# Float32r stacks written by the transfers themselves instead of staged and copied by ScalarE, in a six-attention kernel

## Chip, cores and metric

One NeuronCore of a Trainium2 chip runs the whole kernel. The metric is device time in microseconds (us), the median of several executions. 16 sequences (`B`) of 256 tokens with 256 features go through six attention blocks, 0 to 5, one after the other.

## What is computed

Each block has 16 heads of width 16. In block 0 the scores of queries and keys get two masks; blocks 1, 4 and 5 are plain; block 2 is causal; blocks 2 and 3 count, per head, the non-zero scores of query 0 and mask all keys from that count on (the penalty). The core of blocks 2 and 3 in the reference:

```python
energy = jnp.einsum('bhsk,bhtk->bhst', Q, K)
lengths = jnp.sum(energy[:, :, 0, :] != 0, axis=-1)
energy = jnp.where(cols[None, None, None, :] >= lengths[:, :, None, None], -jnp.inf, energy)
if causal:
    energy = jnp.where(cols[None, :] > cols[:, None], -jnp.inf, energy)
score = jax.nn.softmax(energy / jnp.sqrt(jnp.asarray(dk, energy.dtype)), axis=-1)
out = jnp.einsum('bhst,bhtk->bhsk', score, V) * m
```

Around each attention stand projections of queries, keys and values, a residual sum and a layer norm; blocks 1 and 5 have a feed-forward part of width 1024, block 3 one of width 256.

## The kernel before

**Units and steps.** A unit `n` (0 to 95) is one sequence in one block: block `n // 16`, sequence `n % 16`. One global order of steps, made by `plan()` from the tables `PRE` and `POST` (lines 69 to 110) and sorted by time, is followed by all engines: each walks through `win.order` and does its own part of every entry. Time in the tables is counted in steps, eight to a unit, relative to the unit's start `8 * n`; a negative entry is done while earlier units attend. In step `p` of unit `n` stand `nat` of head pair `p` (scores with queries on the partitions, from which VectorE takes the row maximum, L1018) and `st` of the pair seven steps earlier (transposed scores, of which ScalarE takes the exponential into `pt`, L854). `pvg` (L690) multiplies four pairs by the values. The score banks `ps_nat` and `ps_st` exist once each, so a `nat` waits for the last maximum, an `st` for the last exponential. All else shares the three banks of `ps_misc`; `Order` gives each entry a bank, and a bank is taken again only when its reader has emptied it.

**Queries and keys of blocks 1 to 5.** The scores use float32r operands in stacks `q_st` and `k_st`, double-buffered by unit parity, of 64 rows for each head of a pair: every fourth row (`STEP`) a high part, the next ones high and low parts, so that one product gives near float32 precision; of the rows left over, one holds the penalty (`PEN_R`), two the negated row maximum as high and low part (`HI_R`, `LO_R`), which ScalarE's input then has subtracted already. They are made so:

- `pq` and `pk` (L619): projection into a `ps_misc` bank, held until the low part is out.
- ScalarE rounds the bank into `upper` (L801, L804), VectorE writes the remainder into `lower` (`pql`, `pkl`; L955, L958).
- `qin` and `kin`: SyncE issues three transfers of 256 KB each (L439), which place the parts into the staging areas `raw_q`, `raw_k`, float32. There is one staging area each, so `qin` of a unit waits for the copy of the unit before (L435, L437).
- `pen` (L452): the penalty rows, computed by VectorE in `len` from the small product `e0` (L629), go to `raw_k` by two transfers.
- `qcp` and `kcp` (L814, L826): ScalarE copies each staging area into the stack, in two halves of four pairs, and so rounds to float32r. `nat` waits for them (L492, L493).
- `nmt`: the transposed maxima; GpSimd issues two small transfers into rows `HI_R` and `LO_R` of `q_st` (L1130, L1132).

`upper` and `lower` exist once; the `upper` of a unit waits until the transfers of the unit before have read it (L796). The staging areas lie in slots 1 and 2 of `qk0`, which block 0 uses for its own queries and keys, so that the first `row`, `qin` and `kin` of block 1 wait for unit 14 (L422).

## Time and profile before

| | us |
|---|---|
| median of 3 runs | 2823.91 (2817.97 to 2825.75) |
| the profiled execution, own time | 2822.13 |
| its span, first to last instruction | 2820.3 |
| PE busy in the span | 2653.0 |
| VectorE (DVE) busy | 1816.7 |
| ScalarE (ACT) busy | 1554.2 |

PE is TensorE's matmul side and PEld its weight loads; a busy share counts instructions in flight. SPq is SyncE's queue, which only issues transfers. "PEclk" is the granted share of TensorE's full clock. In a listing, "[x <-y]" is idle time x of the engine before the row and what ended it. Between its own time and its span the profiled execution has 1.8 us.

### The profile page before, as it was taken

The numbers are of one execution on the slowest core, as the hardware profiler recorded it, in microseconds if no ns is written. First come the engines' busy times: TensorE is split into PE (matmuls) and PEld (weight loads), VectorE is DVE, ScalarE is ACT, GpSimd is POOL, SyncE is SP. The second block draws the span as 40 slices with busy tenths as digits, with TensorE's granted clock in tenths as the row PEclk, the third lists the DMA queues.
The fourth block names the chain that finished last, engine by engine and source line by source line (L and its number), as shares of the span: only waits on it lengthen the run. The fifth ranks groups of instructions, "written<-read, shape, count | busy, mean of one in ns | idle before, by whom it ended". The sixth has DMA issues, their size and how long they took to land.

```text
span 2820.3 us, 57005 instructions
## 1 busy us (share of the span) xinstructions
PE 2653.0 (94%) x22720; PEld 1958.1 (69%) x22720; DVE 1816.7 (64%) x3629; ACT 1554.2 (55%) x2129; POOL 749.8 (27%) x838
## 2 busy tenths in 40 slices
PE   7999999899999999999998889889999989999999
PEld 5777777567777777766666666666666667777777
DVE  5566666465555565666668888888677775555552
ACT  1333333365555554566656666666676676666653
POOL 0011111133333332332323444554222221111111
PEclk9999999899999999999999999999999999999999
DMA  2210000121111111122222222122322221111210
GB/s 92 81 45 29 25 25 21 57 81 65 54 54 54 54 47 47 55 93 71 79 77 89 85 70 69 64 70 77 107 70 80 71 81 58 62 62 62 73 47 16
DMA packets 138362, 177.67 MB, mean 63 GB/s; under 512 B 51747, under 2 KB 58547, under 8 KB 138036
## 3 DMA queue, kind: packets, MB, share of 16 engines
q1 hardware_dynamic: 92022, 171.25, 16.9%
q0 software_dynamic: 46080, 2.79, 1.2%
q8 instruction: 184, 3.01, 0.4%
q14 instruction: 76, 0.62, 0.1%
HBM read 40.13 MB, written 4.19 MB: 16 GB/s over the span
## 4 chain that ended last, share of the span: by engine, by line
PE 82%; DVE 9%; ACT 5%; issue 3%; DMA 1%; SPq 0%; POOL 0%; ACTq 0%; DVEq 0%
PE ps_pv L690 10%; PE ps_nat L517 10%; PE ps_misc L749 9%; PE ps_misc L619 9%; PE ps_st L538 8%; PE ps_misc L771 7%; PE ps_misc L645 6%; PE ps_misc L722 4%; DVE mx L1018 4%; ACT pt L854 3%; PE ps_nat L521 2%; PE ps_misc L701 2%; PE ps_st L542 2%; PE ps_misc L614 2%; PE ps_misc L739 2%
## 5 line engine op out<-in xcount | busy, mean ns | idle before, releaser
L854 ACT ACTIVATE pt<-ps_st 128x1024 f32<-128x1024 f32 (+1 forms) x768 | 758.5, 988 | 616.3 <-PE ps_st L542 288.9
L1018 DVE TENSOR_REDUCE mx<-ps_nat 128x4 f32<-128x1024 f32 x640 | 781.0, 1220 | 413.4 <-PE ps_nat L517 267.5
L538 PE MATMUL ps_st<-q_st,k_st 64*128 64x256 f32 (+1 forms) x2560 | 326.1, 333 | 69.9 <-ACT pt L854 66.6
L538 PEld LDWEIGHTS ps_st<-q_st,k_st 64*128 64x128 f32 x2560 | 194.8, 188 | 249.7 <-issue 184.9
L690 PE MATMUL ps_pv<-pt,vaug 128*32 128x256 f32 (+1 forms) x6144 | 361.0, 376 | 0.0
L517 PE MATMUL ps_nat<-k_st,q_st 64*128 64x256 f32 (+1 forms) x2560 | 273.8, 290 | 40.9 <-DVE mx L1018 34.6
L1156 POOL TENSOR_TENSOR rstd<-var,half_pow 128x2 f32<-128x2 f32 x144 | 103.1, 716 | 726.3 <-DVE var L905 724.6
L749 PE MATMUL ps_misc<-xF,weights 128*128 128x256 f32 x1152 | 281.3, 387 | 1.8 <-ACT xF L868 1.5
L1130 POOL DMA_DIRECT2D q_st<-negm_hi x160 | 97.7, 611 | 690.3 <-DVE negm_hi L1028 690.3
L1164 POOL TENSOR_TENSOR xn<-xn,tiles 128x512 f32<-128x512 f32 x128 | 163.8, 1280 | 412.7 <-DVE xn L909 412.4
L690 PEld LDWEIGHTS ps_pv<-pt,vaug 128*32 128x32 f32 x6144 | 179.6, 110 | 123.1 <-issue 10.6
L517 PEld LDWEIGHTS ps_nat<-k_st,q_st 64*128 64x128 f32 x2560 | 202.2, 190 | 60.3 <-DVE mx L1018 23.9
L749 PEld LDWEIGHTS ps_misc<-xF,weights 128*128 128x128 f32 x1152 | 209.8, 190 | 47.2 <-issue 12.3
L771 PE MATMUL ps_misc<-weights,hT 128*128 128x256 f32 x1024 | 240.9, 382 | 0.0
L619 PE MATMUL ps_misc<-xT,weights 128*128 128x256 f32 x896 | 229.2, 400 | 1.8 <-ACT xT L871 0.9
L876 ACT ACTIVATE hT<-ps_misc,cols 128x256 f32<-128x256 f32 x288 | 121.0, 471 | 166.7 <-PE ps_misc L749 166.6
L771 PEld LDWEIGHTS ps_misc<-weights,hT 128*128 128x128 f32 x1024 | 188.5, 190 | 27.8
L619 PEld LDWEIGHTS ps_misc<-xT,weights 128*128 128x128 f32 x896 | 169.6, 198 | 31.2 <-ACT xT L871 4.8
L860 ACT ACTIVATE ote<-ps_pv 128x512 f32<-128x512 f32 x192 | 114.7, 598 | 123.8 <-PE ps_pv L690 123.7
L814 ACT ACTIVATE q_st<-qk 128x1024 fp32r<-128x1024 f32 x160 | 168.6, 1054 | 23.7 <-PE ps_st L538 12.8
L826 ACT ACTIVATE k_st<-qk 128x1024 fp32r<-128x1024 f32 x160 | 169.1, 1057 | 8.5 <-issue 8.5
L1165 POOL TENSOR_TENSOR xn<-xn,tiles 128x512 f32<-128x512 f32 x128 | 163.8, 1280 | 10.0
(117 smaller groups left out, 4082.3 us busy)
## 6 DMA issues: line engine op xcount, KB each, us to landing
qk<-upper SPq DMA_DIRECT2D x320, 256.0 KB, 2.5
qk<-lower SPq DMA_DIRECT2D x160, 256.0 KB, 2.6
weights<-in_weights SPq DMA_DIRECT2D x19, 512.0 KB, 4.7
cT<-in_ctx_t SPq DMA_DIRECT2D x32, 256.0 KB, 2.8
cn<-in_ctx SPq DMA_DIRECT2D x32, 256.0 KB, 2.7
xT<-in_x_t SPq DMA_DIRECT2D x16, 256.0 KB, 2.9
xn<-in_x SPq DMA_DIRECT2D x16, 256.0 KB, 2.7
out<-xn SPq DMA_DIRECT2D x16, 256.0 KB, 3.1
```

The costliest lines, as they stand in the source:

```text
L517: return nc.tensor.matmul(ps_nat[:, j, hf, 0:keys], lhs, rhs, start=hf == 0, stop=last)
L538: return nc.tensor.matmul(ps_st[:, j, kh, 0:S - q0], lhs, rhs, start=kh == first, stop=last)
L619: last = nc.tensor.matmul(bank[:, j * S:(j + 1) * S], wv[:, dk, j * P:(j + 1) * P], src[:, dk, :], start=dk == 0, stop=dk == 1)
L645: last = nc.tensor.matmul(bank[:, hf * D:(hf + 1) * D], src[:, dk, hf * P:(hf + 1) * P], wv[:, dk, :], start=dk == 0, stop=dk == 1)
L690: last = nc.tensor.matmul(ps_pv[32 * j:32 * j + 32, c, q0:S], vaug[:, rot, kh, s, :], pt[:, at_p, s % 2, kh * S:(kh + 1) * S - q0], start= ...
L749: last = nc.tensor.matmul(bank[:, c * S:(c + 1) * S], wu[:, dk, ch * P:(ch + 1) * P], xF[:, dk, :], start=dk == 0, stop=dk == 1)
L771: last = nc.tensor.matmul(bank[:, th * D:(th + 1) * D], hT[:, ch, th * P:(th + 1) * P], wd[:, ch, :], start=part == 0 and ch == 0, stop=pa ...
L814: nc.scalar.activation(q_st[:, rot, 4 * i:4 * i + 4, :], raw_q[:, 4 * i:4 * i + 4, :], ACT.Copy).then_inc(q_stacked, 1)
L826: nc.scalar.activation(k_st[:, rot, 4 * i:4 * i + 4, :], raw_k[:, 4 * i:4 * i + 4, :], ACT.Copy).then_inc(k_stacked, 1)
L854: nc.scalar.activation(pt[:, g % PT_SLOTS, :, 0:used], ps_st[:].rearrange("p j a b -> p j (a b)")[:, :, 0:used], ACT.Exp, scale=SCALE).the ...
L1018: last = nc.vector.reduce_max(out, ps_nat[:], AX)
L1164: link(nc.gpsimd.tensor_tensor(x, x, tile2("g" + name), ALU.mult))
```

## The change

The staging areas, the copies `qcp` and `kcp` and the entries `row` are gone. `qin` and `kin` write straight into the stacks, each as two entries `i = 0, 1` of four head pairs (half a unit). For this the weights' column order (`by_slot`) is changed so that the even partitions of the projections belong to one half and the odd ones to the other. A half of `qin` is four transfers: 4 rows of zeros into `HI_R` and `LO_R` (now 31 and 63) and three of 128 KB; a half of `kin` is three of 128 KB. VectorE's low part is written as float32r. The penalty is also placed per half, two transfers each. From unit 18 on each half waits for the last `st` of the same half two units earlier, whose stack it overwrites. `upper` and `lower` become double-buffered and move into the slots of `qk0`. The constant rows of ones are loaded at the start into `hT` (two transfers of 256 KB) and written once to both buffers of both stacks. The maxima, the exponentials, the products and their shapes stay as they are. The tables `PRE` and `POST` are new throughout; here `PRE` of blocks 1 to 5:

```diff
 PRE = {
-    1: [("ldt", 0, -17.8), ("xtr", 0, -16), ("qin", 0, -12.6), ("pq", 0, -9.5), ("pql", 0, -9.45),
-        ("kin", 0, -8.45), ("pk", 0, -6.5), ("pkl", 0, -5.25), ("qcp", 0, -1), ("pvv", 0, -0.9),
-        ("kcp", 0, -0.15), ("qcp", 1, 1.2), ("kcp", 1, 1.5)],
-    2: [("xtr", 0, -15), ("pq", 0, -14), ("pql", 0, -13.7), ("qin", 0, -9.6), ("pk", 0, -9.3),
-        ("kin", 0, -9.1), ("pkl", 0, -9), ("pen", 0, -8.6), ("q0b", 0, -6.8), ("e0", 0, -5.8),
-        ("qcp", 0, -5.75), ("len", 0, -5.5), ("kcp", 0, -2.5), ("qcp", 1, -2.1), ("kcp", 1, 0.45),
-        ("pvv", 0, 0.5)],
-    3: [("ldn", 0, -20.3), ("xtr", 0, -14.8), ("ctr", 0, -14.3), ("pq", 0, -10.5), ("qin", 0, -9.95),
-        ("pql", 0, -9.7), ("kin", 0, -9.4), ("pk", 0, -9.15), ("pkl", 0, -8.8), ("pen", 0, -7.2),
-        ("q0b", 0, -7), ("e0", 0, -6.3), ("len", 0, -5.75), ("qcp", 0, -4.1), ("kcp", 0, -3.3),
-        ("qcp", 1, -1.7), ("kcp", 1, 1.1), ("pvv", 0, 1.5)],
-    4: [("xtr", 0, -12.4), ("pq", 0, -11.2), ("pql", 0, -9.8), ("qin", 0, -9.6), ("pk", 0, -9.4),
-        ("pkl", 0, -9), ("kin", 0, -7.35), ("qcp", 0, -6.1), ("kcp", 0, -2.6), ("qcp", 1, -1.6),
-        ("kcp", 1, 0.75), ("pvv", 0, 2.5)],
-    5: [("ldn", 0, -22.7), ("clnA", 0, -17.8), ("clnB", 0, -16.9), ("ctr", 0, -14.3), ("xtr", 0, -10.5),
-        ("pq", 0, -9.8), ("pql", 0, -9.7), ("pk", 0, -9.2), ("pkl", 0, -8.6), ("kin", 0, -6.4),
-        ("kcp", 0, -2), ("qin", 0, -1.35), ("qcp", 0, -1.2), ("pvv", 0, 0), ("kcp", 1, 1.1), ("qcp", 1, 3)],
+    1: [("ldt", 0, -17.8), ("xtr", 0, -15.95), ("pq", 0, -10.2), ("pql", 0, -9.8), ("pk", 0, -9.6),
+        ("pkl", 0, -8.6), ("kin", 0, -7.9), ("qin", 0, -4.3), ("kin", 1, -1.5), ("qin", 1, -0.6),
+        ("pvv", 0, 0.1)],
+    2: [("xtr", 0, -15), ("pq", 0, -10.5), ("pql", 0, -9.8), ("pk", 0, -9.8), ("q0b", 0, -9.3),
+        ("pkl", 0, -8.9), ("e0", 0, -8), ("len", 0, -7.2), ("qin", 0, -6), ("kin", 0, -5.4),
+        ("pen", 0, -4.9), ("qin", 1, -1.55), ("kin", 1, -1.5), ("pen", 1, -1.4), ("pvv", 0, 0.8)],
+    3: [("ldn", 0, -17.8), ("xtr", 0, -14.8), ("ctr", 0, -14.3), ("pq", 0, -10.7), ("pql", 0, -9.8),
+        ("pk", 0, -9.6), ("pkl", 0, -9.55), ("q0b", 0, -8.1), ("e0", 0, -8), ("len", 0, -7.2),
+        ("qin", 0, -5.5), ("pen", 0, -5.1), ("kin", 0, -2.6), ("kin", 1, -2.5), ("pen", 1, -2.4),
+        ("qin", 1, -2.3), ("pvv", 0, 1.5)],
+    4: [("xtr", 0, -13.6), ("pq", 0, -10.6), ("pk", 0, -9.6), ("pql", 0, -9.5), ("pkl", 0, -8.85),
+        ("kin", 0, -8.4), ("qin", 0, -6), ("qin", 1, -1.6), ("kin", 1, -1.5), ("pvv", 0, 1.5)],
+    5: [("ldn", 0, -23.7), ("clnA", 0, -18.1), ("clnB", 0, -17.9), ("ctr", 0, -14.3), ("xtr", 0, -12),
+        ("pq", 0, -10.5), ("pql", 0, -9.8), ("pk", 0, -9.6), ("pkl", 0, -8.9), ("qin", 0, -6.2),
+        ("kin", 0, -3.1), ("kin", 1, -1.5), ("qin", 1, 0.1), ("pvv", 0, 0.4)],
 }
...
+        if a == 4 and n % B < 2:
+            for i in range(2):
+                add(8 * n + 4 * i - 5, "pen", n, i)
```

`POST` has the same entries as before at times moved by at most 2.5 steps (block 2: `lnA` 19.2 to 21.7, `lnB` 22.55 to 23.1; block 3: `otr` 0 12.1 to 14.1, `lnB` 1 27.2 to 29.2, `ff1` 24 to 24.5; block 4: `opr` 21.2 to 20.3, `otr` 1 17.5 to 17.95). The buffers and SyncE's part:

```diff
-        raw_q, raw_k = qk0[:, 0, 1:3].rearrange("p r c s -> p (r c) s"), qk0[:, 1, 1:3].rearrange("p r c s -> p (r c) s")
-        lower = sb("lower", [P, 2, 2 * S])
-        bias_b = lower[:, 0].bitcast(BF16)
+        upper = qk0[:, 0, 1:3].rearrange("p r (k c) s -> p r k (c s)", k=2)
+        lower = qk0[:, 1, 1:3].rearrange("p r (k c) s -> p r k (c s)", k=2)
...
+                for c in range(2):
+                    sp.dma_start(hT[32 * c:32 * c + 32], t["rows"][c]).then_inc(rows_loaded, 16)
...
                     elif kind in ("qin", "kin"):
+                        if n >= B + 2:
+                            sp.wait_ge(st_done, nth(("st", n - 2, 4 * i + 3)))
+                        elif n == B and i == 0:
+                            sp.wait_ge(rows_in, 64)
+                        hi, lo = (part[i:P:2, rot, 0 if kind == "qin" else 1] for part in (upper, lower))
                         if kind == "qin":
                             wait_out(sp, ("pq", n, 0))
-                            dst, parts, done = raw_q, (upper[:, 0].bitcast(F32), upper[:, 0].bitcast(F32), lower[:, 0]), q_in[rot]
+                            dst, parts, done = q_st[:, rot, 4 * i:4 * i + 4].bitcast(F32), (hi, hi, lo), q_in[rot][i]
+                            if n == B and i == 0:
+                                sp.wait_ge(zeros_made, 1)
+                            sp.dma_start(dst[HI_R:P:LO_R - HI_R], zeros[:].unsqueeze(1).to_broadcast([4, 4, S])).then_inc(done, 16)
                         else:
                             wait_out(sp, ("pk", n, 0))
-                            dst, parts, done = raw_k, (upper[:, 1].bitcast(F32), lower[:, 1], upper[:, 1].bitcast(F32)), k_in[rot]
-                        if n == B:
-                            sp.wait_ge(st_done, nth(("st", B - 2, PAIRS - 1)))
-                        elif kind == "qin":
-                            sp.wait_ge(q_stacked, nth(("qcp", n - 1, 1)))
-                        else:
-                            sp.wait_ge(k_stacked, nth(("kcp", n - 1, 1)))
+                            dst, parts, done = k_st[:, rot, 4 * i:4 * i + 4].bitcast(F32), (hi, lo, hi), k_in[rot][i]
                         for part, src in enumerate(parts):
                             sp.dma_start(dst[part:P:STEP], src).then_inc(done, 16)
...
                     elif kind == "pen":
                         sp.wait_ge(pen_ready, nth(("len", n, 0)))
+                        if n >= B + 2:
+                            sp.wait_ge(st_done, nth(("st", n - 2, 4 * i + 3)))
                         for m in range(2):
-                            sp.dma_start(raw_k[PEN_R:P:GROUP, m:PAIRS:2], pens[SLOT * m:SLOT * m + 2 * QUADS]).then_inc(pen_in[rot], 16)
+                            sp.dma_start(k_st[PEN_R:P:GROUP, rot, 4 * i + m:4 * i + 4:2].bitcast(F32),
+                                         pens[SLOT * m + QUADS * i:SLOT * m + QUADS * i + QUADS]).then_inc(pen_in[rot][i], 16)
```

TensorE and ScalarE:

```diff
                     if attention(n) > 0 and p % 4 == 0:
-                        pe.wait_ge(q_stacked, nth(("qcp", n, p // 4)))
-                        pe.wait_ge(k_stacked, nth(("kcp", n, p // 4)))
+                        pe.wait_ge(q_in[n % 2][p // 4], placed("qin", n, p // 4))
+                        pe.wait_ge(k_in[n % 2][p // 4], placed("kin", n, p // 4))
+                        if ("pen", n, p // 4) in win.place:
+                            pe.wait_ge(pen_in[n % 2][p // 4], penned(n, p // 4))
...
-                        dst = upper[:, "pq pk".split().index(kind), :]
-
-                        if n > B and kind == "pq":
-                            act.wait_ge(q_in[(n - 1) % 2], placed("qin", n - 1))
-                            if count := nth(("q0b", n - 1, 0)):
+                        dst = upper[:, rot, "pq pk".split().index(kind)].bitcast(F32R)
+                        if n < B + 2:
+                            last_use = max(m for m in range(B) if m % ROT == 1 + rot)
+                            act.wait_ge(st_done, nth(("st", last_use, PAIRS - 1)))
+                        else:
+                            for h in range(2):
+                                if kind == "pq":
+                                    act.wait_ge(q_in[rot][h], placed("qin", n - 2, h))
+                                else:
+                                    act.wait_ge(k_in[rot][h], placed("kin", n - 2, h))
+                            if kind == "pq" and (count := nth(("q0b", n - 2, 0))):
                                 act.wait_ge(q0_ready, count)
-                        elif n > B:
-                            act.wait_ge(k_in[(n - 1) % 2], placed("kin", n - 1))
...
-                    elif kind == "qcp":
-
-                        if i == 0:
-                            act.wait_ge(q_in[rot], placed("qin", n))
-                            if n == B:
-                                act.wait_ge(rows_in, 32)
-                        if n >= B + 2:
-                            act.wait_ge(st_done, nth(("st", n - 2, 4 * i + 3)))
-                        nc.scalar.activation(q_st[:, rot, 4 * i:4 * i + 4, :], raw_q[:, 4 * i:4 * i + 4, :],
-                                             ACT.Copy).then_inc(q_stacked, 1)
-                    elif kind == "kcp":
-
-                        if i == 0:
-                            act.wait_ge(k_in[rot], placed("kin", n))
-                            if n == B:
-                                act.wait_ge(rows_in, 32)
-                            if ("pen", n, 0) in win.place:
-                                act.wait_ge(pen_in[rot], penned(n))
-                        if n >= B + 2:
-                            act.wait_ge(st_done, nth(("st", n - 2, 4 * i + 3)))
-                        nc.scalar.activation(k_st[:, rot, 4 * i:4 * i + 4, :], raw_k[:, 4 * i:4 * i + 4, :],
-                                             ACT.Copy).then_inc(k_stacked, 1)
```

## Rows read from the trace of the kernel before

**Rows 1.** Part 1 of the page, engine busy us (share) xinstructions:

```profile
PE 2653.0 (94%) x22720; PEld 1958.1 (69%) x22720; DVE 1816.7 (64%) x3629; ACT 1554.2 (55%) x2129; POOL 749.8 (27%) x838
```

**Rows 2.** Windows, one per block: stretch, us, busy by engine, PEclk, DMA share, GB/s:

```profile
48.20:557.30 509.10, 488.40 (x4843) 347.35 (x4843) 300.52 (x524) 174.75 (x207) 67.52 (x61) 0.98 0.13 41
557.30:1099.00 541.70, 521.57 (x3848) 393.89 (x3850) 324.78 (x616) 301.32 (x446) 171.40 (x182) 1.00 0.17 58
1099.00:1494.00 395.00, 365.09 (x3949) 276.44 (x3948) 266.29 (x697) 229.38 (x310) 117.64 (x137) 1.00 0.21 71
1494.00:1910.40 416.40, 371.12 (x3104) 262.34 (x3100) 355.06 (x765) 267.00 (x345) 200.80 (x211) 0.95 0.22 74
1910.40:2274.10 363.70, 338.77 (x2886) 240.12 (x2884) 266.83 (x476) 254.51 (x322) 104.03 (x129) 0.96 0.25 84
2274.10:2820.30 546.20, 534.12 (x3939) 414.92 (x3935) 278.53 (x521) 324.89 (x503) 84.49 (x114) 1.00 0.16 56
```

**Rows 3.** Costliest groups, the page: what the change removes on ScalarE, query side:

```profile
L814 ACT ACTIVATE q_st<-qk 128x1024 fp32r<-128x1024 f32 x160 | 168.6, 1054 | 23.7 <-PE ps_st L538 12.8
```

**Rows 4.** Chain of waits in block 3: start, us, what:

```profile
1541.55 0.44 PE ps_misc L701 x4
...
1542.10 0.44 PE ps_st L538 x4
...
1542.77 1.92 PE ps_misc L762 x8
```

**Rows 5.** Window over unit 14's end and unit 15, columns as in 2:

```profile
507.40:557.30 49.90, 42.99 (x255) 25.89 (x254) 17.64 (x33) 16.73 (x24) 7.00 (x7) 0.76 0.20 74
```

**Rows 6.** Timeline at the change from block 0 to block 1:

```profile
512.61 0.84 ACT L801 ACTIVATE upper<-ps_misc,cols 128x256 fp32r<-128x256 f32 x2 [6.65 <-DMA qk<-lower]
...
514.58 1.97 PE L645 MATMUL ps_misc<-weights,cT 128*128 128x256 f32 x8 [3.15 <-DVE lower L955]
...
517.97 0.39 PE L517 MATMUL ps_nat<-k_st,q_st 64*128 64x256 f32 x2 [1.43 <-ACT k_st L826]
```

**Rows 7.** Window of one middle unit of block 1, columns as in 2:

```profile
706.70:741.80 35.10, 34.16 (x250) 26.02 (x249) 20.96 (x39) 19.14 (x30) 11.41 (x12) 1.00 0.16 54
```

**Rows 8.** Timeline of the same unit, its one longer wait on TensorE:

```profile
719.53 0.63 PE L710 MATMUL ps_misc<-ident,on 128*128 128x128 f32 x4 [0.88 <-DVE xn L1103]
```

**Rows 9.** Window of one middle unit of block 2, columns as in 2:

```profile
1245.00:1267.50 22.50, 20.64 (x242) 15.46 (x243) 15.67 (x43) 13.74 (x18) 6.78 (x9) 1.00 0.22 74
```

**Rows 10.** Timeline of block 2: two exponentials with a short step between:

```profile
1259.92 0.81 ACT L854 ACTIVATE pt<-ps_st 128x768 f32<-128x768 f32 x1 [0.58 <-PE ps_st L543]
...
1262.10 0.81 ACT L854 ACTIVATE pt<-ps_st 128x768 f32<-128x768 f32 x1 [1.37 <-PE ps_st L543]
```

**Rows 11.** Window of one middle unit of block 3, columns as in 2:

```profile
1616.60:1643.80 27.20, 24.33 (x202) 17.34 (x198) 23.37 (x52) 17.05 (x23) 13.45 (x15) 0.94 0.20 71
```

**Rows 12.** Timeline of the same unit: a row maximum on VectorE, and who waits:

```profile
1634.01 1.21 DVE L1018 TENSOR_REDUCE mx<-ps_nat 128x4 f32<-128x1024 f32 x1
...
1635.37 0.50 PE L517 MATMUL ps_nat<-k_st,q_st 64*128 64x256 f32 x4 [1.82 <-DVE mx L1018]
```

**Rows 13.** Windows of two middle units of block 4, columns as in 2:

```profile
2091.80:2113.20 21.40, 20.06 (x182) 14.04 (x178) 15.74 (x27) 15.52 (x21) 5.63 (x8) 1.00 0.22 76
2068.80:2091.80 23.00, 21.65 (x182) 15.21 (x178) 15.68 (x27) 15.45 (x20) 5.55 (x8) 0.93 0.21 72
```

**Rows 14.** Timeline of block 4: TensorE waits for a row maximum:

```profile
2186.27 0.50 PE L517 MATMUL ps_nat<-k_st,q_st 64*128 64x256 f32 x4 [0.51 <-DVE mx L1018]
```

**Rows 15.** Chain of waits at the start: start, us, what:

```profile
8.82 4.81 DMA nonzero<-in_pad
...
16.93 2.34 DMA qk<-xF
```

**Rows 16.** SyncE's placing transfers: duration ns min/median/max, first and last start:

```profile
L439 SPq DMA_DIRECT2D qk<-upper x320: 529/584/1992, 506.2 to 2717.9; - x160
```

**Rows 17.** Transfers, part 6 of the page: xcount, KB each, us to landing:

```profile
qk<-upper SPq DMA_DIRECT2D x320, 256.0 KB, 2.5
```

112 lines of the change are left out of this document (57 added, 55 removed).

## The prediction

> **What bounds the kernel now.** I read the busy shares first. TensorE is busy 2653.0 of 2820.3 us, ScalarE 1554.2 [rows 1]. So the change takes work off an engine that is idle 45% of the time, and can pay only where TensorE waits. All of TensorE's idle time is 167 us.
>
> Then one window per block [rows 2]. TensorE is idle 20.7 us in block 0, 20.1 in block 1, 29.9 in block 2, 45.3 in block 3, 24.9 in block 4, 12.1 in block 5; the rest, 14, lies ahead of them. The second thing to see there is the granted clock: 0.95 in block 3 and 0.96 in block 4. The clock has two levels, 2.4 and 1.2 GHz, so a mean of 0.96 over 363.7 us is 14.5 us of full-rate time not given, and 0.95 over 416.4 us is 20.8. Both are losses beside the idle time, and they go only if the waits ahead of them go.
>
> Then one middle unit of each block, because within a block the units repeat almost to the hundredth. Block 1: 35.10 us, TensorE idle 0.94 [rows 7]. Block 2: 22.50, idle 1.86 [rows 9]. Block 3: 27.20, idle 2.87, VectorE busy 23.37 [rows 11]. Block 4: two kinds, 21.40 at clock 1.00 and 23.00 at 0.93, with the same idle time [rows 13]; the difference of 1.6 us is the price of one fall of the clock. Last, the listings inside a unit tell who is late.
>
> A step has some 0.7 us of scores in TensorE (0.44 for `st` [rows 4] and about half of that for `nat`) and whatever filler the tables put there: 1.92 us for a projection of eight matmuls, 0.44 for a block of four transposes [rows 4]. A step with little filler is as long as its loop: `st`, exponential, next `st`. In block 2 two exponentials with only one small transpose between stand 2.18 us apart [rows 10].
>
> **The change, part by part.** The sum is made against the profiled execution's own time, 2822.13 us; it lies 1.8 us under the median of 2823.91.
>
> *The copies.* 160 copies of 1.054 us go, 168.6 us [rows 3], and as many on the key side, some 337 us of ScalarE. I cost them at nothing by themselves: TensorE's work hides them. What they can give is an exponential that starts up to 1.05 us earlier, and only in a step without filler. They are therefore contained in the terms by block below.
>
> *Start, +2.5 us.* The chain at the start runs through SyncE's queue: the issue of the padding at 8.82, 4.81 to its use, and the penalty transfer at 16.93 with 2.34 [rows 15]. The two loads of the constant rows are issued ahead of it. At least two issues of 0.53 us [rows 16], 1 us; at most also two landings of 2.5 [rows 17], 6 us. Nearest are the issues plus part of a landing, since loads overlap: 2.5.
>
> *Block 0 to block 1, -8 us.* ScalarE's `upper` waits 6.65 us for the transfers of the unit before; behind it `lower` is late and a bank is not emptied, and TensorE waits 3.15 us for the bank and then 1.43 for a copy [rows 6]. Over the stretch the mean clock is 0.76 [rows 5], 12.0 us of full-rate time lost in 49.9. With double-buffered `upper` and without staging none of these waits has a cause. What is late next: `upper` of units 16 and 17 waits for the last `st` of units 13 and 14, which stands 0.2 steps behind it in the order, and steps of block 0 without filler remain. Bounds 0 and -16.6 (3.15, 1.43 and 12.0). I take -8: 4 of the waits, a third of the clock.
>
> *Block 1, +3 us.* The 0.88 us before `ott` is a wait for VectorE's addition, which empties the same bank [rows 8]. The new table keeps `ff2`, `ott` next to each other, so this stays. The new table puts `pk` behind `pq` with only `ff1` between; with one bank held by `ff2` it needs the bank of `pq`, whose low part follows a maximum of 1.21 us [rows 12]. I take 0.25 us for 12 units; bounds -0.94 and +0.5 per unit, -11 and +6.
>
> *Block 2, +5 us.* I added TensorE's pieces step by step for both tables. Before, three of eight steps are short, and they hold `xtr`, `nmt` and `otr`. After, `e0` and `len` have moved beside `pvv`, `pq` beside `otr`: again three short steps, with `xtr`, nothing and `nmt`. One block of transposes, 0.44 us [rows 4], that was free is now in a full step. 12 units, +5 us. Bounds: -1.86 for 12 units, -22, all idle time gone [rows 9]; upward, one fall of the clock per unit, +20 (second rival).
>
> *Block 3, -13 us.* The longest wait, 1.82 us, ends with a row maximum that VectorE began late [rows 12]: before, `len` stands in the same short step as two parts of layer norms. The new table moves `len` to step 0, beside `ff1`, `e0` and a block of transposes. But VectorE's 23.37 us per unit stay, and the burst of layer norms stays. I take 0.2 us of waits and half of one clock fall, 0.8 (the unit has 0.94 over 27.20, 1.6 us), so 1.0 for 13 units. Bounds: 0, and the unit at VectorE's own work, -3.8 per unit, -50.
>
> *Block 4, -13 us.* Two waits: exponentials behind copies, and maxima, 0.51 us [rows 14]. Before, VectorE's heavy steps 6 and 7 are followed by two short steps of TensorE; after, `pvv` stands in step 1 and only step 0 is short. 0.35 us for 14 units, 5 us, and of the 14.5 us lost to the clock [rows 2] a good half, 8. Bounds 0 and -33 (1.34 of idle for 14 units and 14.5).
>
> *Block 5, 0.* TensorE is idle 12.1 of 546.2 us at full clock, and that holds the end of the kernel, where the last unit has nothing beside it [rows 2]. Bounds -5 and +3.
>
> *SyncE's queue, 0.* `qin` and `kin` are 6 issues of 0.584 us [rows 16], 3.5 us per unit; they become 14, 8.2 us, and in blocks 2 and 3 four penalty transfers instead of two. The shortest unit has 22.5 us. Moved past them on the queue are `ldn`, `ldt` and `store`, none within two steps of its user. The new waits for `st` two units back stand at -6 and -2 steps, where the tables place the transfers anyway; behind them wait only other placings. Each half lands 2.5 us [rows 17] after issue and has two and a half steps or more. In blocks 4 and 1 `kin` 0 waits up to two steps and blocks `qin` 0, which still has six. Cost if the cover goes: third rival.
>
> The Trainium skill (DMA: Bandwidth & Descriptors, Rules for kernel authors) says that two transfers to disjoint partition halves share the same engines and serialize, and advises one. By it the split gains nothing and adds fixed costs; placed this early that changes no term, but it speaks for the third rival, in which a doubled fixed cost comes too late.
>
> *VectorE and GpSimd, 0.* The low part is the same instruction with another output type; GpSimd's two small transfers per half stay.
>
> Sum: +2.5 - 8 + 3 + 5 - 13 - 13 = -23.5; 2822.1 - 23.5 = 2798.6, and I forecast 2799.
>
> **Rivals.**
> *More goes than I take (17%).* The clock falls of blocks 3 and 4 and of the transition vanish, and block 3 comes down to VectorE's work. For it: these falls follow waits that the change removes. Against: VectorE's bursts stay. Block 3 -40, block 4 -28, transition -14, the rest as above, +10: 2750.
> *Slower through the clock in block 2 (13%).* The new table puts two short steps, 1 and 2, one behind the other, 2.18 us each, with a block of transposes in the one and no filler in the other. In block 3 a clock fall follows each unit's long wait [rows 11, 12]; in block 2 none does now (1.00, rows 9). If one follows here, 1.6 us for 12 units, +20, and the new table's spread idle time keeps the falls in blocks 3 and 4: +20 + 2.5 + 3 + 5 - 4 (transition) - 5 (block 4) - 3 (block 3), 2841. It decides from a mean clock under 0.95 in block 2.
> *SyncE late (5%).* A half of a stack lands after its first `nat` wants it. A half late by 1 us, part of one landing of 2.5 [rows 17], in 45 units of blocks 2 to 4: +45 on the sum, 2844. Against: the slack above.
> *Hidden anyway (15%).* TensorE's order of work only moves its idle time: all block terms within a few us of zero, 2818 to 2830.
> *The change does not do what it says* is out: no copy is left in the text of ScalarE's part.
>
> **How the numbers follow.** The forecast has 50%, with its own range 2775 to 2814. About 0.3%, 8.5 us, is what a measurement of this kernel can tell from no change. Faster by more than that: the forecast's 50, the first rival's 17, 3 from the edge of the hidden case, 70%. Within: 12 of the hidden case and 5 of the slower ones' edges, 17%. Slower: 13%. The range 2752 to 2829 leaves out half of the first rival (8%) and most of the slower ones (11%); its ends take in the start's 6 us and half of the lower bounds of blocks 3 and 4.
>
> **What would show it.** The profile after: ScalarE busy 337 us less, TensorE's busy time a little lower by the clock. Start: first exponential 2 to 3 us later. Transition: `upper` waits under 2 us instead of 6.65. Middle units: block 1 35.3, block 2 22.9, block 3 26.2, block 4 21 to 22, block 5 34.1. Block 3's longest wait of TensorE under 1.2 us. SyncE never the last to release a `nat`. Wrong if block 2 gets shorter, if the clock of block 3 stays at 0.95, or if waits for `q_st` or `k_st` transfers appear in TensorE's list.

## The result: slower by 0.4%, outside the range

The changed kernel takes 2835.35 us in the median of 10 runs (2829.52 to 2839.30), the kernel before 2824.47 beside it; the ratio is 1.0038, 95% interval 1.0023 to 1.0053. The profiled execution took 2835.32 us, span 2833.4. Forecast were 2799 and a range of 2752 to 2829. (An execution at a third of the clock, 7643.8 us, which one later sitting of the kernel before had, is left out everywhere.)

Part 1 of the page of the changed kernel answers to [rows 1]:

```profile
PE 2635.8 (93%) x22677; PEld 1940.1 (68%) x22720; DVE 1830.5 (65%) x3630; ACT 1255.3 (44%) x1809; POOL 753.3 (27%) x838
```

ScalarE is 299 us less busy (337 were foretold, the sum of the copies' durations; they overlapped their neighbours in part, and busy time counts an overlap once), TensorE 17. And yet the span is 13.1 us longer. The windows of the changed kernel follow, one per block, columns as in [rows 2]; the first begins with the first exponential:

```profile
58.70:552.90 494.20, 481.43 (x4814) 345.37 (x4859) 303.13 (x527) 171.70 (x205) 67.48 (x61) 0.99 0.12 40
552.90:1099.20 546.30, 520.97 (x3836) 391.89 (x3832) 322.97 (x616) 238.39 (x378) 171.01 (x182) 0.99 0.18 58
1099.20:1520.20 421.00, 371.83 (x3946) 277.46 (x3939) 265.82 (x693) 169.53 (x247) 117.55 (x136) 1.00 0.20 68
1520.10:1942.00 421.90, 364.08 (x3104) 253.81 (x3104) 365.78 (x764) 204.26 (x281) 201.70 (x210) 0.99 0.22 75
1942.00:2289.70 347.70, 326.03 (x2887) 233.13 (x2884) 265.48 (x476) 194.97 (x259) 105.38 (x129) 0.99 0.27 89
2289.60:2833.40 543.80, 532.05 (x3939) 412.23 (x3935) 282.46 (x525) 274.14 (x445) 86.39 (x115) 1.00 0.17 58
```

Held against [rows 2], this is where the time went:

| part | before | after | difference | predicted |
|---|---|---|---|---|
| up to the first exponential | 48.2 | 58.7 | +10.5 | +2.5 |
| block 0, with the passage to block 1 | 509.1 | 494.2 | -14.9 | -8 |
| block 1 | 541.7 | 546.3 | +4.6 | +3 |
| block 2 | 395.0 | 421.0 | +26.0 | +5 |
| block 3 | 416.4 | 421.9 | +5.5 | -13 |
| block 4 | 363.7 | 347.7 | -16.0 | -13 |
| block 5 | 546.2 | 543.8 | -2.4 | 0 |

Two things stand out. Block 2 is 26 us longer, at a clock of 1.00, as before. And the clock of blocks 3 and 4, 0.95 and 0.96 before, is 0.99: what the prediction hoped for there did happen, but in block 3 the idle time of TensorE grew from 45.3 to 57.8 us and more than took it back.

The table compares one execution of each kernel, and its first two rows depend on that. The last unit of block 0 takes 42.99 us before, at a mean clock of 0.72. In the trace of experiment 2, which is the kernel before with two loads more, it takes 35.01 at 0.90, and block 0 with the passage 500.7 instead of 509.1. Its windows in both:

```profile
514.30:557.30 43.00, 38.98 (x198) 23.53 (x198) 16.89 (x32) 15.04 (x21) 7.00 (x7) 0.72 0.13 44
```

```profile
521.60:556.60 35.00, 31.90 (x203) 19.41 (x206) 16.80 (x32) 15.02 (x21) 7.03 (x7) 0.90 0.15 54
```

So up to 8 of the 14.9 us are a fall of the clock that not every execution of the kernel before has.

**Block 2, one unit.** The chain of waits of the changed kernel through the full step 0 of a middle unit, start, us, what:

```profile
1230.29 0.99 PE ps_misc L634 x8
1231.28 0.60 PE ps_misc L706 x4
...
1232.40 0.43 DVE on L1041
...
1232.88 1.99 PE ps_misc L650 x8
```

L634 is `e0`, L706 the transposes of `otr`, L650 the projection `pvv`. In this step TensorE has results in all three scratch banks at once: `e0`'s waits for `len` on VectorE, `otr`'s for the multiplication at L1041, and the third is that of the transposed maxima (`nmt`, L677). `pvv` needs the bank of the second. The timeline of the same stretch gives the wait, and shows what VectorE still has before it when it ends; times are start, duration, and in brackets the idle time before. A duration reaches a little into the next row, because matmuls are pipelined, so what a piece costs TensorE is read from start to start:

```profile
1231.21 0.66 PE L706 MATMUL ps_misc<-ident,ote 128*128 128x128 f32 x4
...
1231.70 0.27 PE L677 MATMUL ps_misc<-ident,mx 128*16 128x128 f32 x1
...
1232.88 1.99 PE L650 MATMUL ps_misc<-weights,xT 128*128 128x256 f32 x8 [0.91 <-DVE on L1041]
...
1233.26 0.40 DVE L962 TENSOR_SCALAR nonzero<-ps_misc 128x256 f32<-128x256 f32 x1
1233.69 0.42 DVE L964 TENSOR_REDUCE length<-nonzero 128x1 f32<-128x256 f32 x1
1234.15 0.35 DVE L965 TENSOR_SCALAR nonzero<-iota,length 128x256 f32<-128x256 f32 x1
...
1234.81 0.50 PE L543 MATMUL ps_st<-q_st,k_st 64*128 64x128 f32 x4
...
1238.30 0.81 ACT L841 ACTIVATE pt<-ps_st 128x768 f32<-128x768 f32 x1 [0.88 <-PE ps_st L548]
...
1239.26 0.49 PE L543 MATMUL ps_st<-q_st,k_st 64*128 64x128 f32 x4 [0.99 <-ACT pt L841]
```

From exponential to exponential the eight steps take 3.49, 2.18, 3.98, 2.64, 2.18, 3.14, 2.26, 2.64 us before and 5.79, 2.18, 2.27, 2.65, 2.18, 3.39, 2.99, 2.65 after, 22.52 and 24.09 in all. Before, the 3.14 is the short step of `otr`, lengthened because the next exponential comes late behind a copy, and the 2.26 holds `pk`. The clean comparison is with the old steps without copies (experiment 4): 3.49, 2.18, 3.98, 2.64, 2.18, 2.18, 2.99, 2.64, 22.28 in all. So the copies' absence saves 0.24 us per unit, and the new steps cost 1.81:

- 0.91 is the wait for the bank.
- About 0.4 is one `otr`, which stood in a short step, free, and now stands beside `pq`. The step of `pq` and `e0` took 3.98 there, that of `pq` and `otr` takes 3.39 here, and `e0` takes 0.99 from its start to `otr`'s (1230.22 to 1231.21).
- 0.09 is the third short step, 2.27 instead of 2.18; it holds nothing between two `st`, and TensorE waits 0.99 us in it.
- Some 0.3 stand beside the wait: from `otr`'s start to the next `st` are 3.60 us, 1.23 more than the 2.37 of experiment 5, and only 0.91 of that is the wait; the pieces no longer run into one another. 0.1 is not assigned.

**The start.** Chain of waits of the changed kernel, against [rows 15]:

```profile
9.21 0.43 SPq L421
...
9.68 9.11 DMA nonzero<-in_pad
18.81 1.38 DVE xF L926
```

The padding is 0.9 us later in issue, as predicted, but its transfer takes 9.11 us to its use where it took 4.81. Behind it the first work begins 5 us later. What that costs depends on the clock: in another kernel with the same start (experiment 5, its padding takes 8.77 us) the first exponential stands at 50.3, only 2.1 us later than before. The other 8.4 us are TensorE's busy time at a lower clock: over the window from 20 us to the first exponential the mean clock is 0.65 here and 0.87 there, and TensorE is busy for 34.75 and 26.45 us.

```profile
20.00:58.70 38.70, 34.75 (x153) 22.92 (x155) 17.18 (x22) 2.49 (x4) 0.05 (x1) 0.65 0.29 69
```

```profile
20.00:50.30 30.30, 26.45 (x155) 17.92 (x155) 16.84 (x21) 2.49 (x4) 0.00 (x0) 0.87 0.31 71
```

### The profile page after: what moved, and what is told of

Same layout as the page of the kernel before. It is cut to its first block, busy times and chain, and to the rows that moved or that the text cites. A ratio compares the mean times of both kernels' runs of the same rounds, so it can differ in the third digit from the quotient of the medians.

```text
span 2833.4 us, 57517 instructions
## 1 busy us (share of the span) xinstructions
PE 2635.8 (93%) x22677; PEld 1940.1 (68%) x22720; DVE 1830.5 (65%) x3630; ACT 1255.3 (44%) x1809; POOL 753.3 (27%) x838
## 4 chain that ended last, share of the span: by engine, by line
PE 77%; DVE 15%; issue 3%; ACT 3%; DMA 1%; SPq 1%; POOL 0%; DVEq 0%; ACTq 0%
PE ps_pv L695 10%; PE ps_nat L522 10%; PE ps_misc L754 9%; PE ps_misc L624 7%; PE ps_st L543 7%; PE ps_misc L776 7%; DVE mx L1007 6%; PE ps_misc L650 5%; PE ps_misc L727 4%; PE ps_misc L706 3%; PE ps_nat L526 2%; ACT pt L841 2%; PE ps_misc L619 2%; PE ps_st L547 2%; PE ps_misc L744 2%
## 5 line engine op out<-in xcount | busy, mean ns | idle before, releaser
L624 PE MATMUL ps_misc<-xT,weights 128*128 128x256 f32 x896 | 220.0, 389 | 0.2
L522 PE MATMUL ps_nat<-qk 17*128 17x256 f32 x1024 | 149.4, 409 | 10.4 <-ACT pt L841 5.4
L813 ACT ACTIVATE qk<-ps_misc 128x512 fp32r<-128x512 f32 x128 | 76.6, 599 | 168.8 <-PE ps_misc L624 168.8
```

Of the source, the lines that this page charges most:

```text
L522: return nc.tensor.matmul(ps_nat[:, j, hf, 0:keys], lhs, rhs, start=hf == 0, stop=last)
L624: last = nc.tensor.matmul(bank[:, j * S:(j + 1) * S], wv[:, dk, j * P:(j + 1) * P], src[:, dk, :], start=dk == 0, stop=dk == 1)
```

## The experiments

Names of entries are those of the tables `PRE` and `POST`. Where "the rest as after" is said, the kernel is the changed one. The ratios are to the kernel before in the same sitting; its medians lay between 2822.6 and 2826.4 us.

**1. The rows of ones loaded late.** The rest as after.

```diff
-                for c in range(2):
-                    sp.dma_start(hT[32 * c:32 * c + 32], t["rows"][c]).then_inc(rows_loaded, 16)
+    add(2.5, "tld", 0, 0)
...
+                    elif kind == "tld" and i == 0:
+                        for c in range(2):
+                            sp.dma_start(hT[32 * c:32 * c + 32], t["rows"][c]).then_inc(rows_loaded, 16)
```

> The changed kernel with one thing moved: the two 256 KB loads of the constant rows are issued behind the padding and the first steps (step 2.5) instead of ahead of them. Theory (the start is paid for the loads that stand ahead of the padding in SyncE's queue: the padding took 9.11 us to its use in place of 4.81, and half clock followed): the padding is used about 5 us after its issue again, the first exponential starts near 48 to 50 us instead of 58.7, the whole is 8 to 10 us shorter than the changed kernel, and nothing else moves. Rival (the start is longer because of the new order of steps in block 0 or the additional VectorE work, not the loads): the first exponential stays above 56 us and the time is within 2 us of the changed kernel.

Measured: 2826.23 us, ratio 1.0006 (0.9994 to 1.0018), 9.1 under the changed kernel, as the theory had it. The padding takes 5.89 us, but the first exponential stands at 52.7, later than the 48 to 50 expected:

```profile
8.81 5.89 DMA nonzero<-in_pad
14.72 1.38 DVE xF L928
```

**2. The opposite: the two loads put in front of the kernel before**, which has no use for them.

```diff
+                for c in range(2):
+                    sp.dma_start(hT[32 * c:32 * c + 32], t["rows"][c]).then_inc(rows_loaded, 16)
```

> The kernel before, with two loads of 256 KB (the constant rows into a buffer that is not read by then) put ahead of the padding in SyncE's queue, as the changed kernel has them, and nothing else. Theory (these loads alone make the start longer): first exponential 3 to 10 us later than 48.2, the whole 3 to 10 us longer than before. Rival (what makes the start longer in the changed kernel is something else): the whole within 2 us of before.

Measured: 2828.87 us, ratio 1.0027 (1.0011 to 1.0043), within the theory. First exponential at 55.9, padding:

```profile
9.68 8.78 DMA nonzero<-in_pad
```

Over all traces of the study: with the loads ahead the padding takes 7.7 to 9.8 us (eight kernels), without them 4.8 to 5.9 (five). By the medians the two loads cost 6 and 9 us by themselves; the interval of experiment 2 alone allows 3 to 12. They don't explain the first exponential's scatter of 49.8 to 59.0 among kernels with the loads ahead (48.2 to 52.7 without them). The mean clock from 20 us to the first exponential goes with it, 0.65 to 0.87 with the loads ahead and 0.70 to 0.82 without; what decides it was not found. The profiled execution here, 2817.29 us, is the fastest of its ten, 11.6 under their median: its block 0 with the passage is 8.4 us shorter than before and its block 4 3.3.

**3. `pvv` ahead of `otr` in block 2**, to take the bank that is still free. The rest as after.

```diff
-        ("pen", 0, -4.9), ("qin", 1, -1.55), ("kin", 1, -1.5), ("pen", 1, -1.4), ("pvv", 0, 0.8)],
+        ("pen", 0, -4.9), ("qin", 1, -1.55), ("kin", 1, -1.5), ("pen", 1, -1.4), ("pvv", 0, 0.05)],
```

> The changed kernel with one entry moved: in block 2 the value projection pvv goes from 0.8 to 0.05, ahead of the transposes otr, so that it no longer takes the bank that otr has filled and VectorE must first empty (TensorE waits 0.91 us for it in each unit). Theory (a wait for a bank, made by the new order while e0 holds one of the three banks): the 0.91 us wait goes, a middle unit of block 2 falls from 24.09 to 23.1 to 23.3 us, the whole by 10 to 13 us. Rival (block 2 is longer because its short steps moved together, whatever the bank): the wait reappears elsewhere in the step and the unit stays above 23.9 us.

Measured: 2839.44 us, ratio 1.0052 (1.0036 to 1.0067); a unit of block 2 24.13 us, its first steps 5.17 and 2.85. The theory failed, the rival held. The wait for a bank goes from 0.91 to 0.34 us and moves to `nmt`, but the next step loses what this one gains, because VectorE's work for `otr`, `nmt` and `len` now falls together ahead of a row maximum. The bank was where the wait showed; that the step was too full for VectorE is what these rows suggest, and experiment 5 tests it.

**4. All steps as before, only the transfers changed.** The changed kernel with the tables of the kernel before (for entries that exist in both).

```diff
-    2: [("xtr", 0, -15), ("pq", 0, -10.5), ("pql", 0, -9.8), ("pk", 0, -9.8), ("q0b", 0, -9.3),
+    2: [("xtr", 0, -15), ("pq", 0, -14), ("pql", 0, -13.7), ("pk", 0, -9.3), ("pkl", 0, -9), ("q0b", 0, -6.8),
...
```

> The transfers straight into the stacks as in the changed kernel, but all other entries at the times that the tables before had (the copies left out; qin, kin and pen per half where the changed kernel has them, or just behind the low part where that is later). Theory (the transfers themselves cost nothing and save a little; the new order of steps costs block 2 its 1.6 us per unit and block 1 its 0.3): middle units are block 1 35.0 to 35.1, block 2 22.4 to 22.5, block 3 26.5 to 27.3, block 4 20.5 to 21.4; with the start still 10 us longer and block 0 to 1 some 10 us shorter the whole is 2805 to 2822, below the changed kernel. Rival (the doubled number of transfers or their waits cost the time): block 2 stays near 24 us per unit and the whole near 2835 or above.

Measured: 2807.90 us, ratio 0.9935 (0.9913 to 0.9957), as the theory had it. Its block 2, for the line 1099.20:1520.20 above:

```profile
1097.80:1489.20 391.40, 364.08 (x3948) 276.05 (x3942) 266.00 (x697) 169.21 (x247) 117.52 (x137) 1.00 0.22 74
```

So the change is two changes of opposite sign. Direct transfers alone gain 17 us in the median (2824.66 to 2807.90), with the slow start still in them; the new steps lose 27 on top. By the traces, new steps against old, blocks 0 to 5: -3.3, +5.0, +29.6, +7.5, -14.3, -1.2.

**5. `e0` and `len` of block 2 back into the empty step 2.** The rest as after.

```diff
-    2: [("xtr", 0, -15), ("pq", 0, -10.5), ("pql", 0, -9.8), ("pk", 0, -9.8), ("q0b", 0, -9.3),
-        ("pkl", 0, -8.9), ("e0", 0, -8), ("len", 0, -7.2), ("qin", 0, -6), ("kin", 0, -5.4),
+    2: [("xtr", 0, -15), ("pq", 0, -10.5), ("pql", 0, -9.8), ("pk", 0, -9.8), ("q0b", 0, -6.8),
+        ("pkl", 0, -8.9), ("e0", 0, -5.8), ("len", 0, -5.5), ("qin", 0, -6), ("kin", 0, -5.4),
```

> The changed kernel with three entries of block 2 at the times they had before: q0b at -6.8, e0 at -5.8 and len at -5.5, so that the count of non-zero scores lies again in step 2, which is otherwise empty, and not in step 0 beside otr, nmt and pvv. Theory (block 2 lost its time because e0 and len were put into step 0: TensorE's 1 us comes on top of a full step, e0 holds a bank so that pvv waits 0.9 us, and the step they left is empty and waits instead): a middle unit falls from 24.09 to 21.7 to 22.3 us, the whole by 20 to 28 us against the changed kernel, to 2808 to 2816. Rival (pq beside otr in step 5 or the direct transfers cost it): the unit stays above 23.2 us.

Measured: 2795.54 us, ratio 0.9917 (0.9890 to 0.9943), 40 us under the changed kernel. The unit came out as the theory had it, the whole lower than its 2808 to 2816. Windows, block 2 of this kernel:

```profile
1089.80:1481.60 391.80, 366.12 (x3946) 277.25 (x3938) 268.28 (x695) 169.37 (x247) 117.20 (x136) 1.00 0.22 73
```

29.2 us less in block 2. A unit takes 21.79 us: step 0 3.49 instead of 5.79, and step 2, now with `e0` in it, 2.28 instead of 2.27. The timeline shows `pvv` without a wait behind `nmt`, and `e0` in a step that is as long as its exponential's loop:

```profile
1279.77 0.60 PE L706 MATMUL ps_misc<-ident,ote 128*128 128x128 f32 x4
...
1280.21 0.27 PE L677 MATMUL ps_misc<-ident,mx 128*16 128x128 f32 x1
...
1280.32 1.89 PE L650 MATMUL ps_misc<-weights,xT 128*128 128x256 f32 x8
...
1282.14 0.50 PE L543 MATMUL ps_st<-q_st,k_st 64*128 64x128 f32 x4
...
1285.53 1.06 PE L634 MATMUL ps_misc<-qk,q0blk 128*32 128x256 f32 x8
```

Of the 2.30 us, 0.99 are `e0`, now free, and 1.23 the stretch from `otr`'s start to the next `st` (2.37 us here), 0.91 of them the bank; 0.08 are not assigned. That shows the cause of block 2: `e0` and `len` in step 0. Of the 40 us another 8 are, in the profiled executions, a first exponential at 50.3 instead of 58.7. The edit touches nothing of the start, so this is not counted as its merit.

**6. and 7. What are the copies worth?** 320 ScalarE copies of 128x1024, which nobody reads, as many as the change removed: once in the changed kernel, at its `qin` and `kin` entries, once in the kernel of 4, at the very places of the old `qcp` and `kcp`.

```diff
+                    elif kind in ("qcp", "kcp"):
+                        if dead:
+                            act.wait_ge(dead_done, dead)
+                        nc.scalar.activation(scratch[:], tiles[:, 0:4], ACT.Copy).then_inc(dead_done, 1)
+                        dead += 1
```

> The changed kernel with 320 copies of 128x1024 put back on ScalarE, at the entries qin and kin, which read a constant tile and write a buffer that nobody reads. It measures what taking the copies off ScalarE is worth. Theory (ScalarE is covered by TensorE's work, only exponentials in short steps feel a copy): plus 0 to 10 us in all, most of it in block 4, where a middle unit goes from 20.2 to 20.3 to 21.0. Rival (the copies were a real cost which the new order of steps hides by losing elsewhere): plus 20 to 40 us, block 2 over 24.5 and block 4 over 21.3 per unit.

> The kernel of the old-steps run with 320 dead copies of 128x1024 on ScalarE at exactly the places where the copies stood before (qcp, kcp). The difference to the old-steps run is what the removed copies were worth under the old order. Theory (they stood where TensorE had filler, so they cost little): plus 2 to 8 us, block 2 22.3 to 22.5, block 4 21.3 to 21.4. Rival (copies cost much anywhere, as the 37 us of dead copies in the changed order suggest): plus 20 us or more.

Measured: in the changed kernel 2872.63 us, ratio 1.0159 (1.0134 to 1.0185), 37 us more; at the old places 2814.07 us, ratio 0.9976 (0.9963 to 0.9990), 6 us more than without by the medians, 6.8 by the blocks of the traces, 12 by the two ratios (whose intervals allow 4 to 19). The first came out as its rival had it, though block 4's units stayed at 20.54 us; the second, by the medians, as its theory had it. The group of the dead copies on ScalarE, first in the changed kernel, then at the old places:

```profile
L822 ACT ACTIVATE scratch<-tiles 128x1024 fp32r<-128x1024 f32 x320 | 338.9, 1059 | 1.9
```

```profile
L811 ACT ACTIVATE scratch<-tiles 128x1024 fp32r<-128x1024 f32 x320 | 337.9, 1056 | 1.0
```

338 us of work on ScalarE cost 2 to 4% of themselves where an order had been found for them, and 11% where they fell by chance; 25 of those 37 us are block 2 (445.9 us), where the copies stand ahead of exponentials of short steps: TensorE's waits of `st` for `pt` there are 43.3 us instead of 29.5. So ScalarE's own time is the smaller part of what direct transfers gain: by the traces 6.8 of 20.5 us in the six blocks. With the old steps block 0 and the passage take 497.5 us without copies and 497.4 with the dead ones, against 509.1 in the kernel before, so these 11.6 us are not the copies' own time. Unit 14 gives 4.7 of them (36.16 to 31.47 us); in the trace of experiment 2, with the staging areas, it takes 35.75, and its `upper` still waits 6.23 us, so some 4 us are the staging areas that no transfer and no `upper` has to wait for any more. Unit 15 gives 6.9 (42.99 to 36.11), but takes 35.01 in experiment 2 with the staging areas in place: this part is the fall of the clock in one execution, and that the staging causes it is not shown.

**8. A mixed kernel.** Rows late, blocks 0, 4 and 5 with the new steps, 1 and 3 with the old ones, 2 as in 5.

```diff
-    1: [("ldt", 0, -17.8), ("xtr", 0, -15.95), ("pq", 0, -10.2), ("pql", 0, -9.8), ("pk", 0, -9.6),
+    1: [("ldt", 0, -17.8), ("xtr", 0, -16), ("pq", 0, -9.5), ("pql", 0, -9.45), ("pk", 0, -6.5),
...
-    3: [("ldn", 0, -17.8), ("xtr", 0, -14.8), ("ctr", 0, -14.3), ("pq", 0, -10.7), ("pql", 0, -9.8),
+    3: [("ldn", 0, -20.3), ("xtr", 0, -14.8), ("ctr", 0, -14.3), ("pq", 0, -10.5), ("pql", 0, -9.7),
...
```

> A version put together by block: the changed kernel with the constant rows loaded behind the padding, the changed tables for blocks 0, 4 and 5, the tables of before (adapted as in the run with the old steps) for blocks 1 and 3, and block 2 with e0 and len in step 2. Theory (the blocks' costs are separate and add): block 0 30.37, block 1 35.07, block 2 21.7 to 22.3, block 3 27.2, block 4 20.2, block 5 34.1 us per middle unit; against the old-steps run (2808) 9 us less at the start, 6 in block 0, 12 to 16 in block 4 and 0 to 6 in block 2: 2770 to 2785, faster than both kernels. Rival (a gain in one block is paid in the next, because units of two blocks overlap for two units at each border): 2795 to 2808.

Measured: 2782.73 us, ratio 0.9863 (0.9841 to 0.9885), within the theory's 2770 to 2785. Blocks 1 to 4: 542.2, 386.8, 417.9, 347.3.

**9. The same with block 3 laid out anew**: the changed kernel's block 3 (so `lnB` 1 at 29.2), but `e0`, `len` and the first `pen` in the step of 4. The diff, cut, is against the kernel of 8.

```diff
-        ("q0b", 0, -7), ("e0", 0, -6.3), ("len", 0, -5.75), ("qin", 0, -5.5), ("pen", 0, -5.1),
+        ("q0b", 0, -8.1), ("qin", 0, -5.5), ("e0", 0, -4), ("len", 0, -3.8), ("pen", 0, -3.7),
...
-        ("lnA", 1, 26.2), ("lnB", 1, 27.2),
+        ("lnA", 1, 26.2), ("lnB", 1, 29.2),
```

> The mixed kernel (late row loads, the old steps in blocks 1 and 3, the new ones in 0, 4 and 5, block 2 with e0 and len in step 2), and now block 3 with its small pieces moved as well: q0b 1.1 steps earlier, e0, len and the first penalty row in the step of 4, otr 0 and lnB 1 two steps later. In the mixed kernel a unit of block 3 takes 27.31 us, with TensorE idle for 2.7 us of it, all in waits for VectorE. Theory A (what a step costs is the sum of TensorE's pieces in it or of VectorE's, whichever is more, so that moving small VectorE and TensorE pieces out of a full step into an emptier one pays): the unit comes down by 0.6 to 1.0 us, the stage of 418 by 10 to 15, the whole to about 2770 (2767 to 2775). Theory B (in block 3 the wait is set by VectorE's total, 23.4 us of 27.2, and reappears in another step): the unit stays at 27.2 to 27.4 and the whole between 2779 and 2785.

Measured: 2788.44 us, ratio 0.9871 (0.9847 to 0.9894); block 3 takes 424.1 us. Both theories missed: the whole is above either range. The units alternate between 26.54 us at a clock of 1.00 and 28.16 at 0.94. Beside a unit of the changed kernel's block 3, 27.22 at 1.00, the first is 0.68 shorter, which is what theory A asks of the pieces; the fall of the clock in every second unit, 1.6 us, took more than that back.

**10. and 11. `lnB` 1 of block 3 two steps earlier**, in the kernel of 5 and in that of 9.

```diff
-        ("xff", 0, 23.15), ("ff1", 0, 24.5), ("ff2", 0, 25), ("lnA", 1, 26.2), ("lnB", 1, 29.2),
+        ("xff", 0, 23.15), ("ff1", 0, 24.5), ("ff2", 0, 25), ("lnA", 1, 26.2), ("lnB", 1, 27.2),
```

> The changed kernel with e0 and len of block 2 in step 2, and, in block 3, lnB 1 at 27.2 (its place in the kernel before) in place of 29.2. At 29.2 it stands next to lnB 0 of the unit behind it (21.5 + 8 = 29.5), so that VectorE runs four normalizing operations of 256 columns in a row, and the last of them takes 1.39 us beside GpSimd's addition, which began just ahead of it, where one alone takes 0.37; over block 3 these operations take 44.5 us against 33.5 in the kernel before. Theory A (the four in a row are why block 3 gained nothing: the long one delays the row maxima on VectorE, for which TensorE waits 1.6 us): the mean of these operations in block 3 falls from 561 to about 430 ns, block 3 gets 8 to 16 us shorter than 421, the whole 2779 to 2788. Theory B (the long operation is covered, block 3 is set by the step that holds pq, pk and the maxima): the mean falls but the stage stays at 417 to 421 us, the whole 2791 to 2796.

> The mixed kernel with the emptied step filled in block 3 (e0 at -4, len at -3.8), and lnB 1 of block 3 at 27.2 in place of 29.2, beside e10: its stage of block 3 took 424 us with lnB 1 at 29.2, although no four normalizing operations stood in a row there (mean 423 ns). Theory A of e10 says nothing of it except that a part of the layer norms moves one step earlier, away from the maxima of the steps of 29 to 31: 0 to 8 us less in block 3, the whole 2781 to 2788. Theory B: the stage stays within 3 us of 424, the whole 2785 to 2791.

Measured: 2813.94 us, ratio 0.9950 (0.9932 to 0.9968), and 2772.70 us, ratio 0.9806 (0.9789 to 0.9822). By the medians the same edit costs 18 us in the one kernel and gains 16 in the other (by the ratios 9 and 18; in block 3 of the traces 13.3 and 9.0). Both theories missed in both. In 10 the mean of the normalizing operations did not fall (590 ns), and block 3 went from 420.9 to 434.2 us; in 11 block 3 fell by 9.0 us where at most 8 were expected, and the whole lies 8 us under the range. Windows of step 5 of a middle unit of block 3, columns as in [rows 2], first of 10, then of 11:

```profile
1657.50:1663.50 6.00, 4.65 (x20) 3.42 (x21) 3.63 (x7) 1.58 (x3) 5.59 (x7) 0.72 0.11 29
```

```profile
1641.60:1645.30 3.70, 2.86 (x16) 2.03 (x16) 3.60 (x7) 1.55 (x3) 2.96 (x4) 1.00 0.00 1
```

In 10 TensorE waits 1.39 us in this step for a row maximum and runs on at a mean clock of 0.72: the fall of the clock that the new steps had removed from block 3 is back. In 11 the waits of the same steps are 0.75 and 0.49 us in two steps, and the clock is full. The windows of block 3 of both, same order:

```profile
1480.90:1915.10 434.20, 380.42 (x3104) 266.45 (x3104) 358.37 (x768) 204.87 (x280) 201.53 (x211) 0.94 0.22 73
```

```profile
1470.60:1885.70 415.10, 366.31 (x3104) 256.42 (x3104) 359.93 (x767) 204.13 (x280) 201.42 (x211) 0.99 0.23 76
```

TensorE is idle 53.8 us in the first and 48.8 in the second; 14 of the 19 us between them are TensorE's busy time at a lower clock.

The tables of block 3 in experiments 5, 9, 10 and 11 differ in two things only (the first `pen` goes with `e0` and `len`), so the four can be read as a square. Us of block 3:

| `e0` and `len` | `lnB` 1 | experiment | block 3 | TensorE idle | TensorE busy | clock |
|---|---|---|---|---|---|---|
| at -8 and -7.2 | 29.2 | 5 | 420.9 | 58.3 | 362.6 | 1.00 |
| at -8 and -7.2 | 27.2 | 10 | 434.2 | 53.8 | 380.4 | 0.94 |
| at -4 and -3.8 | 29.2 | 9 | 424.1 | 50.2 | 373.9 | 0.96 |
| at -4 and -3.8 | 27.2 | 11 | 415.1 | 48.8 | 366.3 | 0.99 |

Each move alone takes idle time away, `e0` and `len` 8.1 and 5.0 us, `lnB` 4.5 and 1.4. What it then costs or gains is the clock: TensorE's busy time is between 363 and 380 us for the same work. What decides the falls was not found.

Kernel 11 is the best of the study: 1.9% under the kernel before and 2.2% under the changed one.

## Why the prediction was wrong, step by step

- **Block 2 is the step that failed.** "One block of transposes, 0.44 us, that was free is now in a full step" was right: the block is there, and costs about 0.4 us. What the count left out is that a step is not only a sum of TensorE's pieces. I had written that `e0` and `len` moved beside `pvv`, and counted `e0` as one piece among equals in both tables. I did not ask who empties the banks: `e0` holds one until `len`, `otr` one until L1041, and `pvv` is third. That wait is outside the term: the list of waits below has 10.9 us for it in 12 units and 2.7 in four more, 13.6 of the 26. A middle unit grew by 1.57 us, the sixteen of the block by 1.09 to 3.14, the most where the clock fell once. The term was +5; measured +26 (experiment 5 takes 29 away by moving these pieces alone). The upper bound of +20 was put for the wrong reason (a clock fall) and was still too low.
- **The rival "slower through the clock in block 2" did not happen.** Its sign and, within 6 us, its time were right, its mechanism not: the clock of block 2 is 1.00, where it asked for under 0.95. The two short steps one behind the other cost nothing.
- **The start** was put at +2.5 with bounds of 1 and 6. The issues were right (0.9 us), the landing not: I took the loads to overlap with the padding and bounded them by two landings of 2.5 us, one behind the other. Measured are 4 to 5 us more for the padding, and some 6 to 9 us in the whole (experiments 1 and 2). That the padding lands so much later behind the two loads was the missing size. The rest of the +10.5 in the profiled execution is its clock, which scatters from execution to execution (0.65 to 0.87); its cause stays open.
- **Block 0 and the passage**: -8 taken, -14.9 measured. Units 14 and 15 gave 10.7 (36.17 and 42.99 us to 32.22 and 36.24), within the bounds; but 6.8 of that is unit 15, which an execution with the staging areas also does in 35.01 (experiment 2), so the size owes part to the execution that the term was read from. The other 4 come from units of block 0 that went from 30.81 to 30.37 us through the new steps, which the prediction didn't cost at all.
- **Block 1**: +3 taken, +4.6 measured; the middle unit 35.38 against 35.3 foretold, the wait before `ott` still 0.88 us.
- **Block 3**: -13 taken, +5.5 measured. Half of the term was the clock, and that came in full: 0.95 to 0.99. The other half was shorter waits, and these grew by 12.5 us. In a middle unit the two cancel: TensorE's busy time went from 24.33 us to 23.35, its idle time from 2.87 to 3.85, and the unit stays at 27.2 where 26.2 was foretold:

```profile
1650.00:1677.20 27.20, 23.35 (x198) 16.32 (x198) 23.86 (x52) 13.04 (x19) 13.64 (x15) 1.00 0.22 72
```

  The 5.5 us are at the block's borders and in one fall of the clock. I had noted that `len` moves beside `ff1` and `e0` and took it for a relief; it is the same crowding as in block 2 (`ff2`, L767, waits for `len`'s L962, 0.3 us in 12 units), and moving both away takes 5.0 to 8.1 us of idle time out of the block (the square above). Which placing brings the falls of the clock stays open; the expectations of 9, 10 and 11 missed them.
- **Block 4**: -13 taken, -16.0 measured, middle units 20.21 us with 0.68 us idle and no fall of the clock. The mechanism was the predicted one, the gain of the clock larger than a good half: 12.7 us of busy time, 3.3 of waits. Another execution of the old block 4 took 360.4 us instead of 363.7 (experiment 2), so 3 of the 16 may be scatter. With the old steps block 4 gains only 1.7 us (experiment 4), so it is the new table and not the copies.
- **Block 5, SyncE's queue**: 0 and 0 taken; -2.4 and nothing measured. The rival "SyncE late" is out: the halves of `k_st` land in 2.1 us, and the list of TensorE's waits names no transfer of SyncE into a stack:

```profile
PE ps_st L543 <- ACT pt L841: 64.0, 91, 1.2
PE ps_nat L522 <- DVE mx L1007: 37.7, 56, 1.6
PE ps_misc L715 <- DVE xn L1094: 12.3, 14, 0.9
PE ps_misc L650 <- DVE on L1041: 10.9, 12, 0.9
...
PE ps_st L543 <- DMA q_st<-maxm_lo: 4.8, 3, 2.1
...
PE ps_misc L767 <- DVE nonzero L962: 4.1, 12, 0.3
...
PE ps_misc L650 <- DVE maxm_lo L1020: 2.7, 4, 0.7
```

Columns are us in total, times, longest. The fourth line is the wait of block 2, 12 times 0.9 us; the kernel before has it once. The one line with a transfer into a stack is GpSimd's `maxm_lo`, three times. The Trainium skill (DMA: Bandwidth & Descriptors, Rules for kernel authors) says that two transfers to disjoint partition halves serialize, and advises one transfer instead. These runs don't contradict it: 128 KB land in 2.1 us and 256 KB in 2.5 [rows 17], so a half costs nearly as much as a whole, and it changed no time because nothing waited for it.

- **The sum.** Of seven terms four came out within the bounds taken (blocks 0, 1, 4, 5 together -18 taken, -28.7 measured; that block 0's -14.9 is so large owes part to one execution). Three failed upward: start by 8, block 2 by 21, block 3 by 18.5, 47.5 in all.
